# Convolution units in longer blocks, a second accumulator bank, and small steps in other slots of a four-layer kernel

## What is computed

```python
x = _L0_conv_ref(x, ...)  # channel attention: softmax(max - q q^T) q, then se * x + (1 - se) * out
x = _L1_conv_ref(x, ...)  # 1x1 reduce, depthwise 3x3, norm, relu, FFT; 8-head channel attention; gated filter; 1x1
x = _L2_conv_ref(x, ...)  # group norm, 8-head self-attention over 256 pixels, projection, residual
x = _L3_conv_ref(x, ...)  # three 3x3 convolutions q, k, v; softmax over the 16 images per pixel; norm, relu, 3x3, residual
return x
```

## Time and profile before

| | us |
|---|---|
| median of three runs | 513.82 (513.09 to 513.91) |
| profiled execution, its own time | 512.71 |
| its span, first to last instruction | 510.9 |
| TensorE busy | 478.0 |
| VectorE busy | 349.3 |
| ScalarE busy | 252.3 |
| GpSimd busy | 135.0 |

### The profile page before, as it was taken

The page is one execution under the profiler, slowest core; times in us unless marked ns, Lnnn a source line. Parts: engine busy times, 40 slices in busy tenths (PEclk is TensorE's granted clock), DMA queues, the critical chain, the costliest instruction groups (busy, mean ns, idle before and its releaser), DMA issues.

```text
span 510.9 us, 10674 instructions
## 1 busy us (share of the span) xinstructions
PE 478.0 (94%) x3846; PEld 383.0 (75%) x3846; DVE 349.3 (68%) x889; ACT 252.3 (49%) x594; POOL 135.0 (26%) x161
## 2 busy tenths in 40 slices
PE   8698999989999999999999999989997999997896
PEld 7585877667687767876876778677766789896896
DVE  1618857895769677877868696778558342776895
ACT  4233675664555454646455554635435431194551
POOL 6320574261114102210221041021102011252662
PEclk9989999999999999999999999999999999999999
DMA  6000111100000000000000000000000000005012
GB/s 224 22 21 3 47 46 23 46 23 22 0 1 22 22 1 21 21 0 0 21 21 0 0 21 0 1 21 2 1 1 22 1 22 1 1 1 165 24 60 82
DMA packets 9488, 13.20 MB, mean 26 GB/s; under 512 B 496, under 2 KB 8816, under 8 KB 9328
## 3 DMA queue, kind: packets, MB, share of 16 engines
q1 hardware_dynamic: 9456, 12.76, 7.7%
HBM read 8.57 MB, written 4.19 MB: 25 GB/s over the span
## 4 chain that ended last, share of the span: by engine, by line
PE 68%; DVE 17%; ACT 6%; issue 4%; POOL 2%; DMA 1%; DVEq 0%; ACTq 0%
PE bank L1223 9%; PE bank L1225 7%; PE bank L1224 7%; PE bank L1424 5%; PE bank L1398 4%; PE bank L1342 4%; PE bank L1230 3%; PE bank L1374 3%; PE bank L1396 2%; DVE even L898 2%; DVE nmax L998 2%; PE bank L1452 2%; PE bank L1411 2%; PE bank L1247 2%; PE bank L1439 1%
## 5 line engine op out<-in xcount | busy, mean ns | idle before, releaser
L1223 PE MATMUL bank<-win,w_hi 128*128 128x256 f32 x384 | 120.2, 313 | 7.2 <-DVE k L1040 2.3
L1225 PE MATMUL bank<-win,w_lo 128*128 128x256 f32 x384 | 108.2, 282 | 0.0
L1224 PE MATMUL bank<-win,w_hi 128*128 128x256 f32 x384 | 108.1, 282 | 0.0
L749 ACT ACTIVATE prob<-bank 128x512 f32<-128x512 f32 x128 | 69.6, 597 | 72.0 <-PE bank L1396 71.2
L998 DVE TENSOR_REDUCE nmax<-bank 128x2 f32<-128x512 f32 x128 | 85.3, 684 | 20.2 <-PE bank L1374 19.8
L1223 PEld LDWEIGHTS bank<-win,w_hi 128*128 128x128 f32 x384 | 72.5, 189 | 17.8 <-DVE k L1040 3.6
L1224 PEld LDWEIGHTS bank<-win,w_hi 128*128 128x128 f32 x384 | 72.8, 190 | 0.5
L1225 PEld LDWEIGHTS bank<-win,w_lo 128*128 128x128 f32 x384 | 72.4, 189 | 0.0
L528 POOL TENSOR_TENSOR first<-first 128x256 f32<-128x256 f32 x24 | 17.7, 738 | 168.1 <-ACT first L638 168.1
L1230 PE MATMUL bank<-ones_r 128*128 128x256 f32 x316 | 53.6, 307 | 1.1 <-DVE ones_r L852 1.1
L1230 PEld LDWEIGHTS bank<-ones_r 128*128 128x128 f32 x316 | 43.2, 198 | 5.4 <-issue 1.1
(11 more groups left out here) (240 smaller groups left out, 926.6 us busy)
## 6 DMA issues: line engine op xcount, KB each, us to landing
w_stage<-convs SPq DMA_DIRECT2D x4, 576.0 KB, 3.8
x_in<-x SPq DMA_DIRECT2D x8, 256.0 KB, 2.7
out<-x_pair SPq DMA_DIRECT2D x8, 256.0 KB, 2.2
q<-out SPq DMA_DIRECT2D x1, 2048.0 KB, 8.2
out<-v SPq DMA_DIRECT2D x8, 256.0 KB, 2.1
cst<-small SPq DMA_DIRECT2D x1, 1712.0 KB, 9.9
cst<-small SPq DMA_DIRECT2D x1, 253.5 KB, 2.9
```

The costliest lines, as they stand in the source:

```text
L749: act.activation(prob[:, x // 4 % 2, x % 4, :, :], bank[ST_BANK[x % 2]][:, :], ACT.Exp, scale=L2_SCALE).then_inc(st_exp, 1)
L1223: mm(dst, hi, x_hi, start=(row == 0), stop=False)
L1224: mm(dst, hi, x_lo, start=False, stop=False)
L1225: return mm(dst, lo, x_hi, start=False, stop=(row == KH - 1))
```

## The change

- The units of a pair stand in fewer and longer blocks: in the call behind the windows 3, 3, 3, 3, 3, 1, 2 in slots 13, 15, 17, 19, 21, 22, 23; in the next call 6 each in slots 0, 3 and 6.
- Group 4 of pairs 0 to 5 goes to bank 3 (`ST_BANK[0]`) in place of bank 7. It waits until VectorE has read quad 0 of k there; group 5 waits for join 1; `scores_t_pair` waits until ScalarE has copied group 4.
- The joins 1 and 2 are issued in slots 2 and 8 of the next call.
- `o0` on TensorE moves from slot 9 to 8, where it stands ahead of the first `scores_t_pair`. Three keep-busy matmuls fewer stand ahead of `even`.
- VectorE: `gate` from slot 6 to 12; both low parts of k in slot 1 (were 3 and 4); windows in slots 3 and 10 (were 8 and 9); the second image's `window_low` too, in slot 12, instead of GpSimd.
- ScalarE: `sum_x` from slot 3 to 5, the copy of v from 3 to 2, `window_high` in slots 8 and 11 (were 10 and 11) and ahead of the slot's exponentials; a slot's small steps now stand ahead of `first_copy`.

```diff
--- before.py
+++ after.py
@@ -61,19 +61,20 @@
 
 EARLY = ("xt", "sum_x", "energy", "e_min", "att0", "att0_inv", "att0t", "o0", "diff0", "hid0", "z0", "se", "x1", "red",
          "taps0", "taps1", "taps2")
-PE_SLOTS = {"xt": 2, "hid1": 3, "z1": 4, "energy": 4, "xht": 5, "dft": 7, "att0t": 7, "o0": 9, "dot1": 9, "even": 11,
+PE_SLOTS = {"xt": 2, "hid1": 3, "z1": 4, "energy": 4, "xht": 5, "dft": 7, "att0t": 7, "o0": 8, "dot1": 9, "even": 11,
             "hid0": 13, "filt": 12, "z0": 14, "patt": 14, "y1": 15, "gsum": 17, "red": 19}
-ACT_SLOTS = {"xr": 0, "xt": 2, "sum_x": 3, "hid1": 3, "z1": 4, "att0": 6, "att0t": 7, "ab": 7, "o0": 11, "even": 11, "att1": 11,
+ACT_SLOTS = {"xr": 0, "xt": 2, "hid1": 3, "z1": 4, "sum_x": 5, "att0": 6, "att0t": 7, "ab": 7, "o0": 11, "even": 11, "att1": 11,
              "hid0": 13, "filt": 13, "z0": 14, "red": 19}
-DVE_SLOTS = {"n2m": 1, "xh": 3, "xht": 5, "e_min": 5, "gate": 6, "att0_inv": 7, "logit1": 9, "att1_n": 12, "post_att": 14,
+DVE_SLOTS = {"n2m": 1, "xh": 3, "xht": 5, "e_min": 5, "att0_inv": 7, "logit1": 9, "att1_n": 12, "gate": 12, "post_att": 14,
              "se": 16, "x2": 16, "x1": 17, "gvar": 17, "xn": 19, "taps0": 20, "taps1": 21, "taps2": 22}
 POOL_SLOTS = {"rn": 1, "squares": 8, "diff0": 12, "grstd": 18}
 SLOTS = 3 * HEADS
 UNITS = 6
 GROUPS = 6
-CONV_NOW = (0, 0, 0, 0, 0, 0, 0, 0, 0, 0, 0, 0, 0, 2, 1, 3, 0, 3, 1, 2, 0, 3, 1, 2)
-CONV_NEXT = (3, 3, 0, 3, 0, 3, 1, 3, 2, 0, 0, 0, 0, 0, 0, 0, 0, 0, 0, 0, 0, 0, 0, 0)
+CONV_NOW = (0, 0, 0, 0, 0, 0, 0, 0, 0, 0, 0, 0, 0, 3, 0, 3, 0, 3, 0, 3, 0, 3, 1, 2)
+CONV_NEXT = (6, 0, 0, 6, 0, 0, 6, 0, 0, 0, 0, 0, 0, 0, 0, 0, 0, 0, 0, 0, 0, 0, 0, 0)
 CONV_LAST = CONV_NOW
+JOIN_SLOTS = {1: SLOTS + 2, 2: SLOTS + 8}
 
 
 def conv_events(now, rest):
@@ -83,21 +84,21 @@
     last = len(both) - 1
     copied = {done[2 * w]: w for w in range(3) if done[2 * w] is not None}
     summed = {min(done[2 * w] + 1, last): w for w in range(3) if done[2 * w] is not None}
-    joined = {min(done[2 * w + 1] + 1, last): w for w in range(3) if done[2 * w + 1] is not None}
+    joined = {max(min(done[2 * w + 1] + 1, last), JOIN_SLOTS.get(w, 0)): w for w in range(3) if done[2 * w + 1] is not None}
     return copied, summed, joined
 
 
 EVENTS, EVENTS_LAST = conv_events(CONV_NOW, CONV_NEXT), conv_events(CONV_LAST, ())
 
-BUSY_AHEAD, BUSY_EVEN, BUSY_PAIR_1 = 14, 5, {s: 3 for s in range(13)}
+BUSY_AHEAD, BUSY_EVEN, BUSY_PAIR_1 = 14, 2, {s: 3 for s in range(13)}
 BUSY_PAIR_0 = {1: 6, 2: 6, 3: 6, 4: 6, **{s: 3 for s in range(5, 16)}, 16: 6, 17: 6, 18: 6, 19: 6}
 BUSY_EARLY = {"xt": 5, "energy": 9, "att0t": 3, "o0": 8, "hid0": 2, "z0": 13, "red": 30}
 BUSY_BOTH = {"hid1": 6, "energy": 2, "xht": 4, "att0t": 3, "dot1": 3, "even": 4, "hid0": 1, "patt": 3, "y1": 12, "gsum": 3, "red": 12}
 BUSY_NORM = 34
 MIX_SLOTS, SPLIT_SLOTS, WLOW_SLOTS = (None, 4, 13), (1, 9, 16), (2, 10, 19)
 MIX3_SLOT, SPLIT3_SLOT, WLOW3_SLOT = 2, 6, 7
-K_LOW_SLOTS, V_SLOT, HEADS_SLOT, PROJECT_SLOT, ONES_SLOT = (3, 4), 3, 4, 5, 5
-WINDOW_SLOTS, ADD_SLOT, RESIDUAL_SLOT, HIGH_SLOTS, LOW_SLOTS = (8, 9), 6, 7, (10, 11), (11, 12)
+K_LOW_SLOT, V_SLOT, HEADS_SLOT, PROJECT_SLOT, ONES_SLOT = 1, 2, 4, 5, 5
+WINDOW_SLOTS, ADD_SLOT, RESIDUAL_SLOT, HIGH_SLOTS, LOW_SLOTS = (3, 10), 6, 7, (8, 11), (11, 12)
 LN_GROUPS = (slice(0, 2), slice(2, N))
 UNITS_END = (2, 3, 3, 3, 7)
 LAG = 1
@@ -366,6 +367,8 @@
                 return ST_BANK[0]
             if isinstance(j, int) and j == PAIRS - 2 and g in (3, 5):
                 return S2_BANK
+            if g == 4 and not (isinstance(j, int) and j > PAIRS - 3):
+                return ST_BANK[0]
             return CONV
 
         def win_slot(j):
@@ -516,12 +519,6 @@
                                    x2[:, :, :].rearrange("p m x -> p (m x)"),
                                    proj_bias[:, :].to_broadcast([P, PX]), ALU.add).then_inc(x2_res_done, 1)
 
-            def window_low(j, m):
-                k = win_slot(j)
-                pool.wait_ge(win_high, 2 * j + m + 1)
-                pool.tensor_tensor(win_lo[k][:, :, m, 1:H + 1, :], windows[:, m, :, :, :],
-                                   win_hi[k][:, :, m, 1:H + 1, :].bitcast(F32), ALU.subtract).then_inc(win_low, 1)
-
             def first_sum(j, w):
 
                 pool.wait_ge(first_copied, 3 * j + w + 1)
@@ -531,8 +528,6 @@
                 for s in range(SLOTS):
                     if s == RESIDUAL_SLOT:
                         residual(j)
-                    if s == LOW_SLOTS[1] and not (isinstance(j, int) and j == 0):
-                        window_low(j - 1, 1)
                     if cj is None and s in WLOW_SLOTS:
                         k = WLOW_SLOTS.index(s)
                         weights_low(k, w_hi[:, k, :], w_lo[:, k, :])
@@ -741,6 +736,8 @@
                         split_weights(SPLIT_SLOTS.index(s), w_hi[:, SPLIT_SLOTS.index(s), :])
                     if isinstance(cj, int) and cj == 0 and s == SPLIT3_SLOT:
                         split_weights(3, w3_hi)
+                    if s in HIGH_SLOTS and before:
+                        window_high(j - 1, HIGH_SLOTS.index(s))
                     if n >= 0 and n % 2 == 0:
                         if n % 4 == 0:
                             after(act, pv_done, 2 * QUADS * j + n // 4 - 1)
@@ -754,12 +751,10 @@
                         h_copy(j, 0)
                     if s == OUT_SLOT + 4 and late is None:
                         window_high(j, 0)
+                    for what, i in parts(ACT_SLOTS, s, early, late):
+                        stage(what, i)
                     for k, w in conv_steps(0, j, cj, s):
                         first_copy(k, w)
-                    if s in HIGH_SLOTS and before:
-                        window_high(j - 1, HIGH_SLOTS.index(s))
-                    for what, i in parts(ACT_SLOTS, s, early, late):
-                        stage(what, i)
                 if late is not None:
                     qk_high_parts(late, "q")
                 o2_copy(j, 2 * QUADS - 1)
@@ -1051,14 +1046,14 @@
                         join_max(j, s // HEADS - 1)
                     if s < 2 * HEADS:
                         row_max(j, s)
-                    if s in K_LOW_SLOTS:
-                        qk_low_parts(j, "k", (K_LOW_SLOTS.index(s),))
+                    if s == K_LOW_SLOT:
+                        qk_low_parts(j, "k")
                     if s in WINDOW_SLOTS and before:
                         make_window(j - 1, WINDOW_SLOTS.index(s))
                     if s == ADD_SLOT and before:
                         add_x2(j - 1, 1)
-                    if s == LOW_SLOTS[0] and before:
-                        window_low(j - 1, 0)
+                    if s in LOW_SLOTS and before:
+                        window_low(j - 1, LOW_SLOTS.index(s))
                     if s == OUT_SLOT:
                         normalise(j, 0)
                     if s == OUT_SLOT + 2:
@@ -1386,6 +1381,7 @@
                     pe.wait_ge(st_exp, 2 * HEADS * j + n)
                 else:
                     pe.wait_ge(k_rows, 2 * j + 2)
+                    after(pe, first_copied, 3 * (j - 1))
                 for k in range(CH):
                     key = slice(m * HW + k * P, m * HW + (k + 1) * P)
                     for low in range(2):
@@ -1468,6 +1464,10 @@
                             after(pe, joined, 3 * j + 2 if g == 5 else 0)
                         elif conv_bank(j, g - 1) == S2_BANK:
                             pe.wait_ge(first_copied, 3 * j + 2)
+                        elif conv_bank(j, g) == ST_BANK[0]:
+                            pe.wait_ge(qk_low, 4 * (j + 2) + QUADS + 1)
+                        elif conv_bank(j, g - 1) == ST_BANK[0]:
+                            pe.wait_ge(joined, 3 * j + 2)
                         elif g % 2:
                             pe.wait_ge(first_copied, 3 * j + g // 2 + 1)
                         else:
```

## The result

The changed kernel takes 508.86 us on the median of four runs (507.12 to 509.06), the kernel before beside it 513.87. The ratio is 0.9883 with a 95% interval of 0.9836 to 0.993. The forecast was 507.0 in a range of 504.0 to 511.5: the likeliest case, 1.9 us too low. The profiled execution took 508.80 us, its span is 507.0 at a mean clock of 0.976.

A forecast was written before the change was run, and what follows sets the result against it. TensorE, busy 94% of the span, was taken as the bound. Four loop pairs at −0.85 us, pair 6 −1.75, pair 7 −0.9 and pair 1 −0.8 make −6.85: 513.82 to 507.0, range 504.0 to 511.5.

The forecast's parts named there:

- The rival in which VectorE becomes the bound: Slots 10 to 13: low parts and gate slowed beside GpSimd make a loop pair +1.05 us, total 516.0; chance 0.10.
- The removed waits: TensorE's waits for join, copy, row maxima and `h_t` go: 0.4, 0.2, 0.35 and 0.3 us a loop pair.
- steps of blocks: Fewer convolution blocks on TensorE lose start and exit steps: 0.35 us in a loop pair, 0.3 in pairs 6 and 7.
- The 0.35 of the row maxima: Moving VectorE's gate from slot 6 to 12 ends the transposes' wait: 0.35 us in each loop pair and pairs 1, 6.
- `sum_x`, `v`, ... nothing either way: Moved small steps, including `sum_x`, `v` and windows, fall in idle time of their engines: no gain or cost.
- Keep-busy and the logit: Ahead of `even`: three matmuls fewer save 0.35 us in pairs 2 to 6, an earlier logit 0.1 more.
- the wait for `prob`: `o0` ahead of the first `scores_t_pair` leaves the exponentials uncovered: TensorE idles, costing 0.65 us per loop pair, bounds 0.5 to 0.8.
- The window step: Slot 10: VectorE's window between two row maxima delays the scores of slot 12; cost 0.1 to 0.5, taken 0.3 us.
- The low part: Slot 12: VectorE's second `window_low` meets GpSimd's `diff0`, delaying slot 13's first units 0.25 us a loop pair, bounds 0 to 0.8.
- The rival in which the waits move on: Exponentials, window step and low part each cost their upper bound: loop pairs net 0, total 511.3 us; chance 0.20.
- Drain at every block: Every removed block saves a TensorE drain: five blocks at 0.3 us in six pairs, 9 us, total 500; chance 0.03.
- The last pairs: Pair 6 −1.75 us and pair 7 −0.9: waits and steps removed, less new waits such as 0.5 for `join_max`.

The follow-up runs named there:

- a1: The changed kernel with the gate back in slot 6 of VectorE; 507.47 us, ratio to the kernel before 0.9873.
- a2: The changed kernel with the second image's low part back on GpSimd; 507.03 us, ratio to the kernel before 0.9876.
- b2: b1 plus ScalarE's moves: `sum_x` in slot 5, copy of v in slot 2, small steps ahead of `first_copy`; 503.76 us.
- b1: The kernel before with only the new unit tables, bank 3 for group 4 with its waits, the joins and k's low parts; 509.55 us.
- e3: The changed kernel with five keep-busy matmuls ahead of `even` again; 507.85 us, ratio to the kernel before 0.9909.
- d1: The changed kernel with `o0` back in slot 9 and the second window in slot 9, no fills; 502.28 us.
- e2: The changed kernel with `o0` back in slot 9, behind the first `scores_t_pair`; 506.95 us, ratio to the kernel before 0.9889.
- e4: The changed kernel with the second window moved from slot 10 to 9; 506.02 us, ratio to the kernel before 0.9871.
- c2: c1 with the second window in slot 7, two units moved from slot 6 to 8, and fewer fills; 500.49 us.
- c1: d1 with keep-busy matmuls in the waits of pairs 6 and 7; 499.61 us, ratio to the kernel before 0.9724.
- e1: The changed kernel with keep-busy matmuls added in the waits of pairs 6 and 7; 505.36 us, ratio to the kernel before 0.9845.
- d2: c2 with pair 1's windows in slots 3 and 9 and keep-busy matmuls ahead of `dot1` in pairs 0 and 1; 495.99 us.

## Why the prediction was right, and where it was not

The total lies 1.9 us from the forecast, and part of that is luck. In the profiles the loop did 2.0 us better than forecast, pairs 6 and 7 did 5.6 worse, 4.0 of it by the clock in pair 6, and pair 1 and what is ahead of it 0.7 better. Inside the loop, too, errors of both signs cancel.

**What bounds the kernel.** Held. In every kernel the loop pair is TensorE's busy time and its waits, 0.1 to 1.5 us, and no edit that only moved VectorE's busy time changed it (a1, a2). The rival in which VectorE becomes the bound, 516.0, found no sign: the second low part and `diff0` did meet, but the low part went first and took 0.68 us. The sum had let `diff0` go first.

**The removed waits.** They are gone, and their prices were right: 0.4, 0.2, 0.35 and 0.3 forecast, 0.40, 0.20, 0.39 and 0.25 measured from start to start (b2 against before). For the edits that b2 holds, the forecast has these and 0.35 for steps of blocks, 1.6 in a loop pair; b2 gives 1.52. That the sum fits is luck, since other terms in it were wrong. The steps of blocks with the small operations beside them are some 0.97, not 0.35 and the 0.1 that the forecast saw at the logit; a wait of 0.70 for `q_max` came that it did not have there. The 0.35 of the row maxima was put down to the gate; the six units in slot 6 earned it, and the gate's own move is worth nothing in the loop (a1). And "`sum_x`, `v`, ... nothing either way" failed: ScalarE's order is worth 0.74 (b2 against b1). Whether it gains anything on the kernel before was not run; the loop pairs there show no wait for `hid`. The new tables bring such a wait, and half of their gain would have gone. The prediction asked whether ScalarE was idle, where it should have asked what stands ahead of `hid` in its queue.

**Keep-busy and the logit.** Forecast at 0.45. In the changed kernel the three matmuls are worth nothing (e3), since the wait of slot 12 swallows them. Where that wait is gone (d1), the pair is 0.58 shorter than b2. Start to start, 0.35 of it is the three matmuls, 0.14 the step at `q_max` (its wait is 0.58 for 0.70; d1 has the gate in slot 12, b2 in slot 6) and 0.18 the step into the units of slot 13, whose weight loads waited for GpSimd's low part in b2; some 0.1 went the other way.

**The costs.** `o0`: the wait for `prob` came as forecast, 0.53 us in the trace. Its price is 0.14 and not 0.65, because with `o0` in its old place the wait for `q_max` is open (0.58, e2). The prediction used this very wait for pair 6 and forgot it in the loop, where covering it is what `o0` earns. The window step: the mechanism was right, the size was not, 0.60 for 0.3. From the scores of slot 10 to those of slot 12 VectorE's path took 2.71 us (203.72 to 206.43) for 2.6, and TensorE needs 2.20 (203.72 to 205.80, and 0.12) for 2.35; that is 0.51 where the sum had 0.25. The other 0.09 lies between products of the scores themselves, whose steps add up to 1.60 us in the changed kernel and 1.51 in e4. The low part: 0 for 0.25.

These add up: +0.08 for the edits of b2, −0.13 for keep-busy and the rest, −0.51 for `o0`, +0.30 for the window, −0.25 for the low part make −0.51, and the loop pair is −1.35 (−1.36 by these terms) where −0.85 stood. Four pairs of it are the 2.0 us by which the loop did better. The rival in which the waits move on had the loop pairs unchanged; they moved on in kind (0.53 for `prob`, 0.51 for the maximum), but not in size.

**Drain at every block.** By this rival five blocks would give 1.5 us a pair on top of the waits. By the rows they and the steps beside them give 0.97, half of it at one block, so neither this nor the 0.35 of the sum was right, and "0.3 a block" is the wrong form: what a block costs depends on what stands beside it. The sum took the block of slot 14 for one beside other full-array work, but it stood between the scores and `hid`; and slot 18 lost one too, where the sum names slot 7. The Trainium skill (TensorEngine Tiling (Array Packing), Key Properties) has the engine drain at a change of tiling mode. The rows agree: removing the block behind `project_out`, between two full-array operations, gave 0.01 us, and the block that c2 adds between two 32-row products cost 0.14.

**The last pairs.** At the full clock pair 6 is 43.34 to 43.36 (e2, e3, a2) against 43.34 forecast. In the profiled execution TensorE fell to 1.2 GHz there. For the other three runs of the changed kernel nothing shows where it fell: their mean clocks are 0.974 to 0.979, but a2's profile has 0.976 and e2's 0.979, both with a full clock in pair 6 and the low stretches in other places. No step of the prediction deals with the clock: its differences are those of a profile at 0.993. In pair 6 it costs 4.0 us for 10.2 us at the lower level; pair 7 with 6.8 us at it is 58.41, and 55.70 without any in c1, which also has fills and the two moves. The prediction named the very waits that stand ahead of the fall, 0.5 for `q_max` and 0.58 for `prob`, and priced them at their length alone.

**Pairs 0 and 1.** −0.92 for −0.8. Ahead of pair 1 −0.60 for 0; no run took this apart. That stretch is 92.1 to 97.6 us in the profiles, in part by how long the clock was low in it, so its 0.60 says little.

**What stays open.** Why the clock falls in pair 6 in some executions and not in others. Nine of the kernels measured here have both waits there with nothing in them; the profile of five shows the fall (the changed kernel, b1, b2, a1, d1), that of four does not (e2, e3, e4, a2). Of the four with something in them (e1 and c1 with fills, c2 and d2 with two units in slot 8 and fills behind `dot1`) none shows it. That is one profile of each, so the fills are the likely cause and not a proven one; the higher mean clocks of c1's and d2's runs point the same way. In pair 7 e1 fell in spite of its fills, and so did d1, with the moved window and `o0` and no fills; c1, c2 and d2, which have both, did not. How much idle time it takes the runs do not show.

## What to carry to other kernels

When a table of issue moves a block of matmuls, list for every engine what its completion now puts ahead of which small step; here an activation of 0.24 us behind 1.3 us of work took a wait of 0.77 us, half of what blocks, banks and ScalarE's order gave together. List too what the moved block had covered: here `q_max`, 0.70 us. A work item that covers a wait has a price only as the difference of two gaps, so look for what its old place and its new place each leave open. And waits of half a microsecond cost their length in the loop pairs here, but two of them, 2 us apart, stood ahead of each fall of the clock in pair 6, though not every such pair of waits was followed by one, and the fall cost 4.0 us in the changed kernel; there, matmuls of ones in the gap are worth a trial.
